# Attention of a graph layer: units taken in pairs, and the edge parts multiplied by their masks on VectorE

## The chip, the cores and the metric

One core of one Trainium2 chip. The metric is the device time of one execution in microseconds (us), the median of several. Engines as the profile names them: PE is TensorE, DVE is VectorE, ACT is ScalarE, POOL is GpSimd, SP is SyncE, which only issues transfers (SPq is its queue).

## The reference

A graph attention layer over 625 nodes and 20,000 edges sorted by their target, and behind it a layer of eight experts, two of them picked for each node, with a shared one. The change touches only the attention of the graph layer:

```python
logits = jnp.einsum('ehd,ehd->eh', q[src], k[dst])
a = logits + dist_attn + path_attn
mx = jax.ops.segment_max(a, dst, num_segments=N)
e = jnp.exp(a - mx[dst])
s = jax.ops.segment_sum(e, dst, num_segments=N)
sa = e / s[dst]
msg = v[src] * sa[:, :, None]
agg = jax.ops.segment_sum(msg, dst, num_segments=N).reshape(N, D)
```

There are 8 heads of 64 columns (D = 512).

## The kernel before

Attention is done densely. For a tile of 126 target nodes and one head, a **unit**, the kernel needs two matrices of 126 x 628 (targets by sources): the exponentials of the logits, and the sums of the edges' own factors (from the two edge inputs) for each pair of target and source. Five tiles times eight heads are 40 units. Their product, divided by its row sum, is the matrix of weights.

**Blocks.** The sums of the edges come from matmuls. Edges are cut into groups of three target nodes, four groups make a block, and there are 53 blocks (WB). For a block VectorE and GpSimd lay out the operands: VectorE makes four one-hots of the edges' sources (L946, 128 x 628 each, `onehot`) and a mask that says to which of a group's three nodes an edge belongs (L950, `mask`); GpSimd multiplies the edge parts by the mask (L926, `R`, in the profile group_weights: 128 partitions x 288 elements in bf16). TensorE multiplies the two (`sums`, L1045, 24 matmuls), ScalarE copies the result out of PSUM (`copied`, L1001) into one of three buffers, and SyncE stores it (L871) to a scratch tensor in HBM. From there SyncE loads each unit's rows (`unit_rows`, L881, sums_in).

**Windows.** The edges of a block come in by four small transfers (L168) into one of 8 slots. Their places in HBM depend on the data, so the issuing engine first loads them from a table into registers, four for a block. Even blocks are issued by SyncE, odd ones by GpSimd between its products (`load`). The first four are issued in the stage before, behind which SyncE issues the load of Wo.

**Units.** `logits` (L1055, for two units at once) on TensorE; `guards` (L959) on VectorE takes the row maximum; `exps` (L1007) on ScalarE; `weights` (L967) on VectorE multiplies sums and exponentials with the row sum, and takes the reciprocal (L970); `norm` (L1012) on ScalarE scales; `turn` (L1067) on TensorE transposes in five pieces; `keep` (L1017) on ScalarE copies them from PSUM; `weighted_sums` (L1077) on TensorE multiplies by the values for two units; `collect` (L975) on VectorE copies the result.

**Order.** Each engine's order is written out by hand and is fixed; engines wait for each other through counting semaphores. The first 14 blocks (`leading`) are summed before the first unit; VectorE lays out 16. From then on `blocks_by` gives 1.3 blocks to each unit until all are done at unit 30. VectorE does, for each unit, weights, at even ones a collect, the next unit's guards, then the next unit's blocks. ScalarE: norm, exps, keep, copies. TensorE: a block's sums, turn, logits or weighted sums, more sums. SyncE: the rows of two units ahead, then for each block a window's load, a wait for the block's copy, its store; in the last ten units also the four loads of W1 (1 MB each). A barrier ends the stage, and the next one starts with Wo.

## Time and profile before

| | us |
|---|---|
| median of 3 runs | 824.91 (824.5 to 826.6) |
| the profiled execution | 826.6 |
| its span, first to last instruction | 825.0 |
| TensorE busy in it | 700.9 |
| VectorE busy | 530.6 |
| ScalarE busy | 418.2 |
| GpSimd busy | 162.0 |

The profile is one execution. The time of an execution lies a little over its span. Times in the views are counted from the span's start. The attention stage lies between about 96 and 323 us; what comes before it prepares the edges and the projections, and what comes after are the feed-forward and the experts.

### The profile page before, as it was taken

The page shows a single profiled execution, that of the slowest core. Times are in us where ns is not written, and L with a number is a line of the kernel's source. Part 1 is how long each engine was busy: PE and PEld are TensorE (multiplying, and loading weights), DVE is VectorE, ACT ScalarE, POOL GpSimd, SP SyncE. Part 2 cuts the span into 40 slices and gives each one's busy share as a digit, 9 for nine tenths or more (in the row PEclk, how much of TensorE's full clock was granted, in tenths as well). Part 3 has the DMA queues.
Part 4 walks back from the last instruction along what each step waited for, and adds up shares of the span by engine and source line. Part 5 has one row for each costly group of instructions (what it writes and reads, how often), then busy time and mean ns, then how long its engine had stood idle before and what let it go on. Part 6 is the DMA issues. An engine that isn't in the chain of part 4 may idle for free. (4 is left out here: it accounts for less than half of the span.)

```text
span 825.0 us, 14610 instructions
## 1 busy us (share of the span) xinstructions
PE 700.9 (85%) x4978; PEld 550.0 (67%) x4978; DVE 530.6 (64%) x1109; ACT 418.2 (51%) x689; POOL 162.0 (20%) x240
## 2 busy tenths in 40 slices
PE   3987766776777764999999999999999999999993
PEld 2664333444555443479999679878889899888792
DVE  6737775788778543544422636338888788888854
ACT  4235333575656653373333543227666676676640
POOL 6341376455544103000000000400000000000022
PEclk9999965999989977999999999999999999999998
DMA  8633545656565581700001040957677677766124
GB/s 263 169 78 74 102 109 165 168 151 178 152 176 166 169 298 28 266 1 1 1 0 62 16 153 1 324 206 257 201 226 235 222 240 237 268 224 227 69 63 144
DMA packets 104157, 125.63 MB, mean 152 GB/s; under 512 B 32402, under 2 KB 70060, under 8 KB 103564
## 3 DMA queue, kind: packets, MB, share of 16 engines
q1 hardware_dynamic: 96955, 115.06, 43.9%
q0 software_dynamic: 5600, 6.54, 3.6%
q10 hardware_dynamic: 1520, 3.01, 1.6%
q8 instruction: 43, 0.70, 0.4%
q14 instruction: 39, 0.31, 0.1%
HBM read 94.91 MB, written 29.67 MB: 151 GB/s over the span
## 5 line engine op out<-in xcount | busy, mean ns | idle before, releaser
L2150 PE MATMUL ps<-xT,w_hi 128*128 128x480 f32 (+7 forms) x512 | 110.1, 337 | 2.3 <-DVE hT L1969 2.2
L2150 PEld LDWEIGHTS ps<-xT,w_hi 128*128 128x128 f32 x512 | 82.0, 189 | 9.9 <-DVE hT L1969 4.0
L1045 PE MATMUL ps<-onehot,group_weights 128*32 128x314 bf16 x1272 | 63.8, 347 | 26.3 <-POOL group_weights L926 8.6
L946 DVE TENSOR_SCALAR onehot<-iota_h,windows 128x628 bf16<-128x628 f16 x212 | 78.8, 433 | 4.1 <-PE ps L1045 4.0
L1955 DVE TENSOR_TENSOR w_lo<-weights_far,w_hi 128x1024 fp32r<-128x1024 f32 x64 | 77.9, 1219 | 2.5 <-ACT w_hi L2065 2.2
L2152 PEld LDWEIGHTS ps<-xT,w_lo 128*128 128x128 f32 x512 | 73.5, 190 | 1.6
L2152 PE MATMUL ps<-xT,w_lo 128*128 128x240 f32 (+7 forms) x512 | 74.5, 268 | 0.0
L1045 PEld LDWEIGHTS ps<-onehot,group_weights 128*32 128x32 bf16 x1272 | 38.6, 113 | 52.1 <-issue 28.4
L2065 ACT ACTIVATE w_hi<-weights_far 128x1024 fp32r<-128x1024 f32 x64 | 67.1, 1051 | 0.0
L168 POOL DMA_DIRECT2D windows<-window_scratch x104 | 58.8, 568 | 36.9 <-issue 30.9
L2175 PE MATMUL ps<-w_hi,hidden 128*128 128x512 f32 (+3 forms) x176 | 62.2, 405 | 2.7 <-DVE hidden L1979 1.9
L1001 ACT ACTIVATE sums_out<-ps 128x628 f32<-128x628 f32 x53 | 36.6, 691 | 46.8 <-PE ps L1045 43.2
L1941 POOL DMA_INDIRECT weights_far<-slot_results,gate x5 | 5.1, 1027 | 269.6 <-DMA slot_results<-weights_near 268.4
L1236 DVE TENSOR_TENSOR ff_hidden_lo<-ff_hidden,ff_hidden_hi 128x628 fp32r<-128x628 f32 x16 | 13.0, 812 | 66.1 <-ACT ff_hidden_hi L1320 66.1
L1067 PE MATMUL ps<-ident,weights 126*128 126x126 f32 (+1 forms) x200 | 33.6, 304 | 23.9 <-ACT weights L1012 22.0
L967 DVE CUSTOM_DVE_ANT_0 weights<-sums_in,exponents 126x628 f32<-126x628 f32 x40 | 33.7, 843 | 30.3 <-DMA sums_in<-sums_scratch 13.9
L926 POOL TENSOR_TENSOR group_weights<-windows,mask 128x288 bf16<-128x288 bf16 x53 | 40.3, 765 | 60.4 <-DVE mask L950 60.1
L1955 DVE TENSOR_TENSOR w_lo<-weights_near,w_hi 128x1024 fp32r<-128x1024 f32 x35 | 42.7, 1221 | 8.1 <-ACT w_hi L2065 8.1
L1012 ACT ACTIVATE weights<-weights,small 126x628 f32<-126x628 f32 x40 | 32.7, 817 | 29.2 <-DVE small L970 29.2
L1067 PEld LDWEIGHTS ps<-ident,weights 126*128 126x128 f32 (+1 forms) x200 | 23.1, 151 | 36.6 <-ACT weights L1012 30.4
L1317 ACT ACTIVATE ff_hidden<-ps,vs 128x314 f32<-128x314 f32 x32 | 16.6, 523 | 58.7 <-PE ps L1412 58.7
L1077 PE MATMUL ps<-weights_turned,vs 128*64 128x126 f32 (+1 forms) x400 | 31.6, 315 | 16.2 <-ACT weights_turned L1017 16.2
(309 smaller groups left out, 1544.6 us busy)
## 6 DMA issues: line engine op xcount, KB each, us to landing
weights_far<-in_L_ffn_w SPq DMA_DIRECT2D x64, 512.0 KB, 5.8
sums_scratch<-sums_out SPq DMA_DIRECT2D x53, 314.0 KB
weights_near<-in_L_ffn_w SPq DMA_DIRECT2D x32, 512.0 KB, 3.4
sums_in<-sums_scratch SPq DMA_DIRECT2D x40, 309.1 KB
weights_near<-in_L_gnn_W SPq DMA_DIRECT2D x4, 1024.0 KB, 6.5
weights_near<-in_L_ffn_sw SPq DMA_DIRECT2D x8, 512.0 KB, 5.1
weights_near<-in_L_gnn_Wqkv SPq DMA_DIRECT2D x3, 1024.0 KB, 7.8
weights_ff<-in_L_gnn_W SPq DMA_DIRECT2D x1, 3072.0 KB, 13.2
```

Of the source, the lines that this page charges most:

```text
L168: eng.dma_start(windows[:, w % RING, j, :], frm.rearrange("(p c) -> p c", p=P)).then_inc(g_in[w % RING], 16)
L926: pool.tensor_tensor(R[w % 3][:, :, 0:GD * H, :].rearrange("p j (d h) a -> p j d (h a)", h=H), parts[:, w % RING, :, 4:4 + 3 * H].unsqueez ...
L946: dve.tensor_scalar(onehot[w % 3][:, j, :], iota_h, windows[:, w % RING, j, 1:2], None, ALU.is_equal)\
L967: dve.tensor_tensor_reduce(PR[k][0:TILE], sums_in[u % 3][0:TILE], L[k][0:TILE], 1.0, 1e-37, ALU.mult, ALU.add, total[k][0:TILE]).then_inc( ...
L1001: act.activation(halves(sums_out[w % 3]), psW(w), ACT.Copy).then_inc(w_copied, 1)
L1045: last = pe.matmul(psW(w)[r, a, :], R[w % 3][:, j, :, part], onehot[w % 3][:, j, a * SH:(a + 1) * SH], start=part == 0, stop=part == 2)
L1067: last = pe.transpose(psP[0:n, t, 0:TILE], PR[u % 2][0:TILE, t * P:t * P + n], ident[0:TILE, 0:TILE])
L1955: dve.tensor_tensor(to[1], raw_rest[n] if v == V else raw[u][n], to[0], ALU.subtract)\
L2065: act.activation(to[0], raw_rest[n] if v == V else raw[u][n], ACT.Copy).then_inc(w_hi_ready, 1)
L2150: pe.matmul(both(bank, cap), w[u % 2][0][:, c, cut], xT(r)[:, c, :, :], start=c == 0, stop=False)
L2152: last = pe.matmul(bank[:, 0:cap], w[u % 2][1][:, c, cut], xT(r)[:, c, 0, :], start=False, stop=c == DC - 1)
L2175: last = pe.matmul(psum[4 + blk][0:rows, :], hid_parts[:, v % 2, m, at:at + rows], w2s[u][wp][:, m, :], start=first and i == 0, stop=final ...
```

## The change

- The product of edge parts and mask is made by VectorE (`products`), with the mask made one step ahead of it (`masks`, `products`, `onehots` in place of `group_weights`). GpSimd only issues its loads.
- The order of all engines goes by pairs of units (`PAIRS`), with 8 blocks to three pairs (`blocks_by`, `pair_blocks`); VectorE lays out two blocks ahead of TensorE (`laid_out`).
- Blocks 2 and 3 of every four are loaded by GpSimd, the others by SyncE (`by_pool`); the places of two blocks, eight registers, are loaded at once (`load_starts`). `place_at` gives the block whose load is issued with block w. Six blocks instead of four are loaded in the stage before.
- A unit's rows have four buffers instead of three, and are asked for by pairs.

```diff
-LOADED = 4
+LOADED = 6
...
-def blocks_by(unit):
-    return min(WB, window_blocks(0) + SPARE_BLOCKS + (13 * unit + 9) // 10)
...
-def unit_blocks(unit):
-    return range(blocks_by(unit), blocks_by(unit + 1)) if unit < UNITS_ALL else range(0)
+def blocks_by(pair):
+    return min(WB, window_blocks(0) + SPARE_BLOCKS + (8 * pair + 2) // 3)
+def pair_blocks(pair):
+    return range(blocks_by(pair), blocks_by(pair + 1))
+def laid_out(pair):
+    return range(min(WB, blocks_by(pair) + 2), min(WB, blocks_by(pair + 1) + 2))
...
...
+PAIRS = UNITS_ALL // 2
+def by_pool(w):
+    return w % 4 >= 2
+def place_at(w):
+    return [b for b in range(LOADED, 2 * WB) if by_pool(b)][w // 2], [b for b in range(LOADED, 2 * WB) if not by_pool(b)][w // 2]
+def load_starts(nc, engine, w, tab):
+    n = min(2 * GW, GROUPS - GW * w)
+    _, starts = nc.values_load_multi_w_load_instructions(tab[0:1, REL + GW * w:REL + GW * w + n], engines=[engine], min_val=0,
                                                          max_val=CHUNK * REC2)
+    return starts
+def load_groups(eng, w, starts, rec2_d, windows, g_in):
     for j in range(min(GW, GROUPS - GW * w)):
         b, k = divmod(GW * w + j, GPB)
         region = rec2_d[b, :, :].rearrange("e c -> (e c)")
-        frm = region[bass.ds(starts[j], P * REC2)] if k else region[0:P * REC2]
+        frm = region[bass.ds(starts[GW * (w % 2) + j], P * REC2)] if k else region[0:P * REC2]
         eng.dma_start(windows[:, w % RING, j, :], frm.rearrange("(p c) -> p c", p=P)).then_inc(g_in[w % RING], 16)
...
-            for w in range(0, LOADED, 2):
-                load_groups(nc, sp, mybir.EngineType.SP, w, tab, rec2_d, windows, g_in)
+            for w in range(LOADED):
+                if not by_pool(w):
+                    starts = load_starts(nc, mybir.EngineType.SP, w, tab) if w % 2 == 0 else starts
+                    load_groups(sp, w, starts, rec2_d, windows, g_in)
             sp.dma_start(wo[:, :, :], Wo.rearrange("(c p) n -> p c n", p=P)).then_inc(wo_in, 16)
...
-            for w in range(1, LOADED, 2):
-                load_groups(nc, pool, mybir.EngineType.Pool, w, tab, rec2_d, windows, g_in)
+            for w in range(LOADED):
+                if by_pool(w):
+                    starts = load_starts(nc, mybir.EngineType.Pool, w, tab) if w % 2 == 0 else starts
+                    load_groups(pool, w, starts, rec2_d, windows, g_in)
...
-        sums_in = [sb(f"sums_in{i}", [P, SRC]) for i in range(3)]
+        sums_in = [sb(f"sums_in{i}", [P, SRC]) for i in range(4)]
...
-            def load(w):
-                if w < WB and w % 2 == 0:
-                    wait_past(sp, windows_stored, stored_for(w))
-                    window_free(sp, w)
-                    load_groups(nc, sp, mybir.EngineType.SP, w, tab, rec2_d, windows, g_in)
-            def blocks(ws):
-                for w in ws:
-                    load(w + AHEAD)
-                    sp.wait_ge(w_copied, w + 1)
-                    sp.dma_start(sums_d[w, :, :], sums_out[w % 3]).then_inc(out_done[w % 3], 16)
+            starts = None
+            def block(w):
+                nonlocal starts
+                nxt = place_at(w)[1]
+                if w % 2 == 0 and nxt < WB:
+                    starts = load_starts(nc, mybir.EngineType.SP, nxt, tab) if nxt % 2 == 0 else starts
+                    wait_past(sp, windows_stored, stored_for(nxt))
+                    window_free(sp, nxt)
+                    load_groups(sp, nxt, starts, rec2_d, windows, g_in)
+                sp.wait_ge(w_copied, w + 1)
+                sp.dma_start(sums_d[w, :, :], sums_out[w % 3]).then_inc(out_done[w % 3], 16)
...
             def unit_rows(u):
                 tile, h = divmod(u, H)
                 if h == 0:
                     for i in range(3):
                         sp.wait_ge(out_done[i], 16 * len(range(i, window_blocks(tile), 3)))
-                wait_past(sp, summed, u - 2)
+                wait_past(sp, summed, u - 3)
                 g0 = tile * TILE // GD
                 rows = sums_d.rearrange("w (j d h) n -> (w j) d h n", j=GW, h=H)
-                sp.dma_start(sums_in[u % 3][0:TILE, :], rows[g0:g0 + TILE // GD, 0:GD, h, :]).then_inc(units_in[u % 3], 16)
...
-            for w in range(LOADED, AHEAD):
-                load(w)
-            blocks(range(window_blocks(0) + 1))
+                sp.dma_start(sums_in[u % 4][0:TILE, :], rows[g0:g0 + TILE // GD, 0:GD, h, :]).then_inc(units_in[u % 4], 16)
+            for w in range(window_blocks(0) + 1):
+                block(w)
             unit_rows(0)
             unit_rows(1)
-            blocks(range(window_blocks(0) + 1, leading))
-            for u in range(UNITS_ALL):
-                if u + 2 < UNITS_ALL:
-                    assert blocks_by(u) >= window_blocks((u + 2) // H)
-                    unit_rows(u + 2)
-                blocks(unit_blocks(u))
-                if UNITS_ALL - 10 <= u < UNITS_ALL - 2 and u % 2 == 0:
-                    load_w1(sp, W1, w_near, [(u - UNITS_ALL + 10) // 2], w1_in)
+            for w in range(window_blocks(0) + 1, leading):
+                block(w)
+            for q in range(PAIRS):
+                if q + 1 < PAIRS:
+                    assert blocks_by(q) >= window_blocks((2 * q + 2) // H)
+                    unit_rows(2 * q + 2)
+                    unit_rows(2 * q + 3)
+                for w in pair_blocks(q):
+                    block(w)
+                if PAIRS - 5 <= q < PAIRS - 1:
+                    load_w1(sp, W1, w_near, [q - PAIRS + 5], w1_in)
...
-            def load(w):
-                if w < WB and w % 2:
-                    wait_past(pool, windows_stored, stored_for(w))
-                    window_free(pool, w)
-                    load_groups(nc, pool, mybir.EngineType.Pool, w, tab, rec2_d, windows, g_in)
+            starts = None
             for w in range(WB):
-                pool.wait_ge(masked, w + 1)
-                wait_past(pool, w_ready, w - 2)
-                pool.tensor_tensor(R[w % 3][:, :, 0:GD * H, :].rearrange("p j (d h) a -> p j d (h a)", h=H),
-                                   parts[:, w % RING, :, 4:4 + 3 * H].unsqueeze(2).broadcast_to([P, GW, GD, 3 * H]),
-                                   mask[w % 2].unsqueeze(3).broadcast_to([P, GW, GD, 3 * H]), ALU.mult).then_inc(r_ready, 1)
-                load(w + AHEAD - 1)
+                nxt = place_at(w)[0]
+                if w % 2 == 0 and nxt < WB and nxt % 2 == 0:
+                    starts = load_starts(nc, mybir.EngineType.Pool, nxt, tab)
+                if w % 2 == 0 and nxt < WB:
+                    wait_past(pool, windows_stored, stored_for(nxt))
+                    window_free(pool, nxt)
+                    load_groups(pool, nxt, starts, rec2_d, windows, g_in)
...
-            def group_weights(w):
+            def masks(w):
                 dve.wait_ge(g_in[w % RING], groups_in(w))
-                wait_past(dve, w_ready, w - 2)
-                for j in range(GW):
-                    dve.tensor_scalar(onehot[w % 3][:, j, :], iota_h, windows[:, w % RING, j, 1:2], None, ALU.is_equal)\
-                       .then_inc(oh_ready, 1)
                 k0 = GW * w % GPB
                 wait_past(dve, r_ready, w - 1)
                 dve.tensor_tensor(mask[w % 2], windows[:, w % RING, :, 0:1].broadcast_to([P, GW, GD]),
                                   offsets[:, k0 * GD:(k0 + GW) * GD].rearrange("p (j d) -> p j d", d=GD), ALU.is_equal)\
                    .then_inc(masked, 1)
+            def products(w):
+                wait_past(dve, w_ready, w - 2)
+                dve.wait_ge(masked, w + 1)
+                dve.tensor_tensor(R[w % 3][:, :, 0:GD * H, :].rearrange("p j (d h) a -> p j d (h a)", h=H),
+                                  parts[:, w % RING, :, 4:4 + 3 * H].unsqueeze(2).broadcast_to([P, GW, GD, 3 * H]),
+                                  mask[w % 2].unsqueeze(3).broadcast_to([P, GW, GD, 3 * H]), ALU.mult).then_inc(r_ready, 1)
+            def onehots(w):
+                wait_past(dve, w_ready, w - 2)
+                for j in range(GW):
+                    dve.tensor_scalar(onehot[w % 3][:, j, :], iota_h, windows[:, w % RING, j, 1:2], None, ALU.is_equal)\
+                       .then_inc(oh_ready, 1)
...
-                dve.wait_ge(units_in[u % 3], 16 * (u // 3 + 1))
+                dve.wait_ge(units_in[u % 4], 16 * (u // 4 + 1))
...
-                dve.tensor_tensor_reduce(PR[k][0:TILE], sums_in[u % 3][0:TILE], L[k][0:TILE], 1.0, 1e-37, ALU.mult, ALU.add,
+                dve.tensor_tensor_reduce(PR[k][0:TILE], sums_in[u % 4][0:TILE], L[k][0:TILE], 1.0, 1e-37, ALU.mult, ALU.add,
...
-            for w in range(2):
-                group_weights(w)
-            guards(0)
-            for w in range(2, blocks_by(1)):
-                group_weights(w)
-            for u in range(UNITS_ALL):
-                weights(u)
-                if u % 2 == 0 and u:
-                    collect(u // 2 - 1)
-                if u + 1 < UNITS_ALL:
-                    guards(u + 1)
-                for w in unit_blocks(u + 1):
-                    group_weights(w)
-            collect(UNITS_ALL // 2 - 1)
+            masks(0)
+            for w in range(leading + 2):
+                products(w)
+                if w in (1, 2):
+                    guards(w - 1)
+                if w + 1 < leading + 2:
+                    masks(w + 1)
+                onehots(w)
+            for q in range(PAIRS):
+                ws = list(laid_out(q))
+                weights(2 * q)
+                if q:
+                    collect(q - 1)
+                weights(2 * q + 1)
+                for w in ws[0:1]:
+                    masks(w)
+                if q + 1 < PAIRS:
+                    guards(2 * q + 2)
+                for w in ws[0:1]:
+                    products(w)
+                    onehots(w)
+                for w in ws[1:2]:
+                    masks(w)
+                if q + 1 < PAIRS:
+                    guards(2 * q + 3)
+                for w in ws[1:2]:
+                    products(w)
+                for w in ws[2:]:
+                    masks(w)
+                for w in ws[1:2]:
+                    onehots(w)
+                for w in ws[2:]:
+                    products(w)
+                    onehots(w)
+            collect(PAIRS - 1)
...
-            for w in range(2):
+            for w in range(leading):
                 copied(w)
-            exps(0)
-            for w in range(2, leading):
-                copied(w)
-            for u in range(UNITS_ALL):
-                norm(u)
-                if u + 1 < UNITS_ALL:
-                    exps(u + 1)
-                keep(u)
-                for w in unit_blocks(u):
+                if w in (1, 2):
+                    exps(w - 1)
+            for q in range(PAIRS):
+                ws = list(pair_blocks(q))
+                norm(2 * q)
+                norm(2 * q + 1)
+                keep(2 * q)
+                for w in ws[0:1]:
+                    copied(w)
+                if q + 1 < PAIRS:
+                    exps(2 * q + 2)
+                keep(2 * q + 1)
+                for w in ws[1:2]:
+                    copied(w)
+                if q + 1 < PAIRS:
+                    exps(2 * q + 3)
+                for w in ws[2:]:
                     copied(w)
     @block.tensor
             logits(0)
             for w in range(leading):
                 sums(w)
-            for u in range(UNITS_ALL):
-                ws = list(unit_blocks(u))
+            for q in range(PAIRS):
+                ws = list(pair_blocks(q))
+                if q + 1 < PAIRS:
+                    logits(q + 1)
                 for w in ws[0:1]:
                     sums(w)
-                turn(u)
-                if u % 2 == 0 and u + 2 < UNITS_ALL:
-                    logits(u // 2 + 1)
-                if u % 2:
-                    weighted_sums(u // 2)
-                for w in ws[1:]:
+                turn(2 * q)
+                turn(2 * q + 1)
+                for w in ws[1:2]:
+                    sums(w)
+                weighted_sums(q)
+                for w in ws[2:]:
                     sums(w)
```

## Rows read from the trace of the kernel before

**Rows 1.** The windows view of two stretches: length, busy PE, PEld, DVE, ACT, POOL, clock

```profile
98.00:139.00 41.00, 23.82 (x360) 13.95 (x364) 27.34 (x80) 10.40 (x15) 30.02 (x48) 0.69 0.59 132
139.00:279.00 140.00, 103.23 (x1453) 69.10 (x1449) 108.86 (x319) 86.13 (x126) 64.60 (x101) 0.92 0.59 166
```

**Rows 2.** The order of time on GpSimd (POOL), leading part; start us, us, instruction

```profile
114.12 1.30 POOL L926 TENSOR_TENSOR group_weights<-windows,mask 128x288 bf16<-128x288 bf16 x2
...
121.40 0.63 POOL L168 DMA_DIRECT2D windows<-window_scratch  x1 [1.51 <-DVE onehot L946]
...
124.34 1.30 POOL L926 TENSOR_TENSOR group_weights<-windows,mask 128x288 bf16<-128x288 bf16 x2
```

**Rows 3.** The order of time on SyncE's queue (SPq), before and in the leading part

```profile
82.45 5.43 SPq L168 DMA_DIRECT2D windows<-window_scratch  x8
...
95.70 2.00 SPq L138 DMA_DIRECT2D window_scratch<-edge_parts  x2
101.65 5.41 SPq L168 DMA_DIRECT2D windows<-window_scratch  x8
...
132.85 0.91 SPq L871 DMA_DIRECT2D sums_scratch<-sums_out  x2
135.33 1.01 SPq L881 DMA_DIRECT2D sums_in<-sums_scratch  x1
```

**Rows 4.** The order of time on VectorE (DVE), the first weights

```profile
139.49 0.81 DVE L967 CUSTOM_DVE_ANT_0 weights<-sums_in,exponents 126x628 f32<-126x628 f32 x1 [3.58 <-DMA sums_in<-sums_scratch]
```

**Rows 5.** The order of time on VectorE (DVE), around unit 29

```profile
275.20 0.29 DVE L975 COPY hT<-ps 128x126 f32<-128x126 f32 x1 [1.43 <-PE ps L1077]
275.41 0.80 DVE L959 TENSOR_REDUCE small<-ps 126x1 f32<-126x628 f32 x1
276.12 1.25 DVE L946 TENSOR_SCALAR onehot<-iota_h,windows 128x628 bf16<-128x628 f16 x4
277.29 0.16 DVE L950 TENSOR_TENSOR mask<-windows,offsets 128x12 bf16<-128x12 f32 x1
277.37 0.80 DVE L967 CUSTOM_DVE_ANT_0 weights<-sums_in,exponents 126x628 f32<-126x628 f32 x1
...
278.45 0.81 DVE L959 TENSOR_REDUCE small<-ps 126x1 f32<-126x628 f32 x1
```

**Rows 6.** Groups of VectorE's instructions by form; count, busy us, mean ns, idle before

```profile
L1969 DVE TENSOR_TENSOR hT<-hT,ps 128x288 f32<-128x288 f32 x8 | 3.5, 443 | 0.0
...
L594 DVE TENSOR_TENSOR edge_parts<-records,edge_parts 128x400 bf16<-128x400 f32 x1 | 1.0, 958 | 0.5 <-ACT edge_parts L692 0.5
```

**Rows 7.** The instructions of line 168 on GpSimd; ns min/median/max

```profile
L168 POOL DMA_DIRECT2D windows<-window_scratch x104: 534/534/1257, 82.9 to 258.3; - x104
```

**Rows 8.** The order of time on SyncE's queue in units 0 to 29

```profile
204.12 0.91 SPq L881 DMA_DIRECT2D sums_in<-sums_scratch  x1
205.98 0.35 SPq L871 DMA_DIRECT2D sums_scratch<-sums_out  x1
208.16 1.88 SPq L168 DMA_DIRECT2D windows<-window_scratch  x4
```

**Rows 9.** The order of time, all engines, units 30 to 39

```profile
280.22 0.81 DVE L967 CUSTOM_DVE_ANT_0 weights<-sums_in,exponents 126x628 f32<-126x628 f32 x1 [0.95 <-ACT exponents L1007]
...
310.35 0.82 ACT L1012 ACTIVATE weights<-weights,small 126x628 f32<-126x628 f32 x1 [0.59 <-DVE small L970]
...
311.22 0.76 PE L1067 MATMUL ps<-ident,weights 126*128 126x126 f32 x5 [0.67 <-ACT weights L1012]
...
312.87 1.30 PE L1077 MATMUL ps<-weights_turned,vs 128*64 128x126 f32 x20 [0.89 <-ACT weights_turned L1017]
...
318.53 1.26 PE L1067 MATMUL ps<-ident,weights 126*128 126x126 f32 x5 [3.15 <-ACT weights L1012]
...
320.58 2.37 PE L1077 MATMUL ps<-weights_turned,vs 128*64 128x126 f32 x20 [0.79 <-ACT weights_turned L1017]
323.00 0.29 DVE L975 COPY hT<-ps 128x126 f32<-128x126 f32 x1 [5.37 <-PE ps L1077]
```

4 lines of the change are left out of this document (1 added, 3 removed).

## Prediction

> **What bounds the kernel now.** I read the busy time by stretches first, then the order of time inside each stretch, since the change lies in one stage that runs from about 97 to 323 us. The stage has three parts with different limits. The first stretch (98 to 139 us) is the leading part: 14 blocks are summed before the first unit. GpSimd is the busiest engine there, 30.02 of 41.00 us, and TensorE was granted 0.69 of its full clock on the mean, so for much of it the lower of its two levels, 1.2 GHz [rows 1]. In the order of time GpSimd repeats itself every 10.22 us (114.12 to 124.34) for four blocks: four products, two bursts of four load issues, and register loads in front of a burst (1.51 us of the gap before 121.40) [rows 2]. It is never idle for long, so it sets 2.56 us a block. SyncE stores block 11 by 133.76 us, issues the first unit's rows at 135.33 [rows 3], and VectorE, idle for 3.58 us, starts the first weights at 139.49 [rows 4].
>
> In the second stretch (units 0 to 29, 139.49 to 280.22, 140.7 us for 30 units and their blocks) no engine is full: VectorE is busy 108.86 of 140.00 us, TensorE 103.23, ScalarE 86.13, GpSimd 64.60 [rows 1]. The time goes into turns between engines: each unit's chain runs alone. In the third (units 30 to 39, no blocks left, 280.22 to 323.29, 43.1 us) only that chain is left [rows 9].
>
> **The change part by part.** *The product moves from GpSimd to VectorE, 53 times.* The trace has no such product on VectorE. The nearest row by size is an addition of 288 elements, 443 ns [rows 6]; an operation starts about 0.09 us before the one in front ends (a reduction of 0.80 us holds the engine for 0.71) [rows 5], so I take 0.36 us. From above: another with two-byte elements and strided operands took 958 ns for 400 elements [rows 6], so 0.69 and 0.60 us of engine. From below: no less than 0.2 us, since the mask with its 12 elements already lasts 0.16 [rows 5]. I choose the 288-element row, since the product reads its parts and writes its result contiguously, as that one does; the other strides. A block then costs VectorE 0.08 for the mask, 0.36, and 1.17 for the four one-hots, 1.61 us [rows 5].
>
> A rule bears on the lower bound. The row says 0.443 us for 288 elements of four bytes, and the product has two. By the Trainium skill (Vector Engine (DVE) Microarchitecture Reference, section 5.1) a two-source operation on two-byte data doubles its rate only if every operand's innermost step is one, and the mask is read with step zero here. By that rule 0.36 stands; at double rate it would be about 0.2, and the sum would fall by 37 times 0.16, 5.9 us.
>
> The product adds two waits on VectorE: for its own mask, with another operation laid between, and for the sums of three blocks before. Behind the second stand the block's one-hots and the next unit's reduction, and ScalarE's exponentials wait for those; three blocks back TensorE is done by then (below).
>
> *Loads.* GpSimd only issues, and runs ahead as slots come free. SyncE has the same number of bursts, but takes eight registers at once for two windows. Now four registers cost the gap from 206.33 to 208.16, 1.83 us; eight cost between that and 3.66; I take 3.0, since part must be per register. A burst of four issues is 1.9, a store 0.45, a unit's rows 0.95 [rows 8].
>
> *Before the stage.* SyncE now ends its window loads at 87.88 and issues Wo. It gets 8 more issues, 3.8 us ((5.43 less some 1.6 for the registers between) over 8 each), 1.2 for a longer first register load, 3.0 for a second: it ends near 96.3, and the stage's first transfer now starts at 95.70 [rows 3]. So the stage starts 1.0 later (0 to 2). Behind these issues stands Wo's load, wanted only after the stage.
>
> *The leading part.* GpSimd leaves the path. VectorE would need 16 blocks of 1.61 and two reductions, 27.2 us, ending near 125 to 126. SyncE is later: its first burst starts at 101.65 plus 1.2 plus 1.0, 103.85; blocks 0 to 3 need two bursts and four stores, 5.6; blocks 4 to 11 twice 3.0 plus 5.6. It issues the store of block 11 by 126.7, against 133.76 now. From there the same 5.73 us to the first weights: 132.4. That is 7.1 us less. With registers at 3.66 and bursts at 2.7 it is 139.2, no gain; with registers at 1.83 and no late start it is 127.9, 11.6 less. What is late next is SyncE, whose stores free the three output buffers.
>
> *Units 0 to 29, in pairs.* By the new order each engine has two units' work between its waits. I laid one pair of three blocks out: weights at 0 and 1.3, reductions at 2.4 and 5.0; ScalarE scales at 1.1 and 2.4, keeps at 3.3 and 5.5, exponentiates at 4.7 and 6.9; TensorE's weighted sums end at 7.5. Every wait of VectorE's is met before VectorE comes to it. So VectorE's own work sets it: 15 pairs of two weights (2.16), a collect (0.21) and two reductions (1.42), 56.9 us, and the 37 blocks not yet laid out at 1.61, 59.6: 116.4 us [rows 5]. TensorE with its 103.23 and ScalarE with its 86.13 fit below. SyncE needs, for four blocks (1.5 pairs), 3.0 + 3.8 + 1.8 + 2.85 = 11.45 us, 115 us in all [rows 8]. Two in-order queues this near to full won't run without gaps: VectorE is idle 22% of this stretch now [rows 1], and I keep half that share: 130 us, 10.7 less. With the product at 0.60 it is 10 us more, at 0.2 about 6 less.
>
> *Units 30 to 39.* The chain that repeats per pair runs from a collect to the next: to the odd unit's weights 0.21, to its scaling's end 1.05 and 0.82, keep of the even unit 0.7, turning of the odd and its keep 1.65 (311.22 to 312.87), weighted sums 1.33: 5.76 us [rows 5, 9]. Four pairs at that, and 8.2 from the last pair's start to its collect, are 31.2 us. At the lower clock turning takes 1.26 for 0.76 and the weighted sums 2.37 for 1.30 [rows 9], 1.57 more a pair; for half of the five pairs, 3.9. So 35.1 us for 43.1, 8.0 less (4 to 11.6). The four loads of W1 lie in this part; a unit's rows are now asked for four units ahead, not three, which covers them.
>
> The fourth sums buffer and the later place of Wo's load cost nothing: both lie beside other work. Behind the stage nothing changes, as a barrier ends it.
>
> Sum: 7.1 + 10.7 + 8.0 = 25.8 us less. The profiled execution took 826.6 us (span 825.0); 800.8 then, and against the median of 824.91, 799.1. I say 800.
>
> **The rivals.**
> *The pairs bring little and the product is dear.* At 0.60 us of engine the second stretch needs VectorE for 116.4 + 37 x 0.24 = 125.3 us, with the same share of gaps 140: no gain there, and 810 us. For it speaks the 958 ns row [rows 6], against it that row's strides.
> *SyncE becomes the bound.* Registers at 3.66, bursts at 2.7: 13.7 us for four blocks, 137 us, and its rows come late; leading part as now. Then only 4 and 8 us are gained: 813. For it speaks that a wait on a copy holds all behind it in SyncE's queue, and that 8 issues with the registers between took 5.41 us at 101.65 [rows 3]; against it, that its registers are fetched half as often.
> *The chains don't overlap in fact* (the change doesn't do what it says): a wait that I didn't see keeps the second and third stretch as they are; only the 7.1 us remain: 818.
> *Slower: GpSimd's load issues starve.* VectorE works with hardly a gap, and GpSimd's issue must get in between. An issue takes 534 ns in the median and 1257 at most today [rows 7]. GpSimd needs 8 issues and some 2.2 us of registers for four blocks. It decides from 1.7 us an issue: then four blocks take 15.8 us, the stretch 158, 17 over now, which eats the other gains. At 2.0 us it is 182 us for the stretch, about 26 us over now in all: 851. Against it: in units 0 to 29 issues lay beside one-hots all the time at 0.53.
>
> On this the Trainium skill (SBUF — State Buffer, Who interferes with whom) says that VectorE's two-port modes lock GpSimd out of writing its descriptors, and the same page (A bandwidth-pool intuition that's wrong) has an issue of about 0.62 us taking about 3.1 beside such a copy; by it the stretch would be near 270 us. The rows, with their maximum of 1.257, don't show it.
>
> **How the numbers follow.** Chances: forecast 0.52; product nearly twice as fast (794 us) 0.08; product dear 0.12; SyncE 0.10; no overlap 0.08; slower 0.06; several of these at once, worth about nothing, 0.04, of it 0.03 within 0.3%. Within the forecast SyncE's registers (7 us) and the clock in the third stretch (4) give 793 to 808. The range must take in the dear product and SyncE as bound, and goes to 816; below, the fast product in part: 792. Under 0.3% (2.5 us) is what a measurement of this kernel can't tell from no change. So faster 0.90, same 0.03, slower 0.07.
>
> **What would show it.** In the profile after: first weights near 132 us, VectorE's product near 0.45 us long, GpSimd under 20% busy in the stage; weights of unit 30 some 130 us after the first, VectorE over 85% busy between; the last collect 35 us later. Wrong it would be by a product over 0.65 us, by SyncE's register load over 3.5 us with VectorE waiting for a unit's rows, by load issues over 1.3 us, or by pairs of more than 7 us in the third stretch.

## Result, and the profile after

The changed kernel takes 817.47 us (median of 5, 812.19 to 819.45) where the kernel before, measured beside it, takes 824.5 (median of 5, 822.4 to 826.6): ratio 0.9895, interval 0.9854 to 0.9936. It is faster by 7 us, not by 25. The profiled execution is the fastest of the five: 812.19 us, span 810.2, against 826.6 and 825.0 before.

Four points in the order of time divide the difference of the spans: first weights, weights of unit 30, last collect, and the first transfer of the stage behind. In short the first four lines are called head, units, tail and gap.

| part | before | forecast | after |
|---|---|---|---|
| to the first weights | 139.49 | 132.4 | 138.32 |
| units 0 to 29 | 140.7 | 130 | 128.6 |
| units 30 to 39, to the last collect | 43.1 | 35.1 | 35.9 |
| last collect to the next stage | 4.7 | 4.7 | 10.8 |
| the rest of the span | 497.0 | 497.0 | 496.5 |

So 1.2 + 12.1 + 7.2 - 6.1 + 0.5 = 14.9 us (the spans differ by 14.8). Two lines of the table are off, the first and the fourth.

The windows view of the kernel after, as [rows 1] (the last two columns are the busy share of the transfer engines and GB/s); the third stretch is units 30 to 39, the fourth the way to the next stage:

```profile
98.00:138.00 40.00, 25.15 (x378) 14.18 (x376) 27.53 (x96) 11.05 (x16) 22.37 (x40) 0.74 0.84 167
138.00:268.00 130.00, 100.79 (x1474) 67.42 (x1474) 113.50 (x359) 88.19 (x129) 33.04 (x56) 0.92 0.62 184
268.00:302.00 34.00, 23.38 (x184) 16.99 (x182) 15.87 (x40) 20.31 (x28) 2.67 (x3) 0.82 0.75 215
302.00:314.00 12.00, 0.84 (x8) 0.42 (x4) 0.35 (x2) 0.32 (x1) 3.48 (x3) 0.50 0.01 2
```

GpSimd falls from 64.60 to 33.04 us in the units, VectorE is busy 113.50 of 130 us, 87%. In the leading part GpSimd falls from 30.02 to 22.37 us, and the transfers' share goes from 0.59 to 0.84. In the last stretch next to nothing is busy for 12 us.

The order of time on SyncE's queue, after, in front of and in the leading part, as [rows 3]:

```profile
94.80 0.43 SPq L451 DMA_DIRECT2D wo<-in_L_gnn_Wo  x1
95.64 4.99 SPq L138 DMA_DIRECT2D window_scratch<-edge_parts  x2
105.10 1.91 SPq L193 DMA_DIRECT2D windows<-window_scratch  x4
107.06 0.90 SPq L901 DMA_DIRECT2D sums_scratch<-sums_out  x2
108.20 2.86 SPq L193 DMA_DIRECT2D windows<-window_scratch  x4
111.11 2.30 SPq L901 DMA_DIRECT2D sums_scratch<-sums_out  x2
116.23 1.87 SPq L193 DMA_DIRECT2D windows<-window_scratch  x4
...
121.33 0.90 SPq L901 DMA_DIRECT2D sums_scratch<-sums_out  x2
126.30 1.88 SPq L193 DMA_DIRECT2D windows<-window_scratch  x4
...
131.34 0.90 SPq L901 DMA_DIRECT2D sums_scratch<-sums_out  x2
133.93 1.88 SPq L911 DMA_DIRECT2D sums_in<-sums_scratch  x2
```

Three things differ from the forecast. The two stores right behind Wo's load hold the queue for 4.99 us instead of 2.00 [rows 3], and the first burst (four window loads) starts at 105.10, not 103.85. The first four blocks take 8.3 us (to 113.41), not 5.6. Registers for eight places cost 2.82 us (113.41 to 116.23) and 4.07 (122.23 to 126.30) against 3.0. The last store is issued by 132.24, forecast 126.7.

VectorE in the order of time, after, as [rows 4]: end of its leading blocks, first weights, weights of unit 30, last collect:

```profile
129.18 1.25 DVE L990 TENSOR_SCALAR onehot<-iota_h,windows 128x628 bf16<-128x628 f16 x4
138.32 0.81 DVE L1006 CUSTOM_DVE_ANT_0 weights<-sums_in,exponents 126x628 f32<-126x628 f32 x1 [7.89 <-DMA sums_in<-sums_scratch]
...
266.96 0.81 DVE L1006 CUSTOM_DVE_ANT_0 weights<-sums_in,exponents 126x628 f32<-126x628 f32 x1 [2.79 <-DMA sums_in<-sums_scratch]
...
302.58 0.29 DVE L1014 COPY hT<-ps 128x126 f32<-128x126 f32 x1 [6.12 <-PE ps L1145]
```

VectorE is done with 16 blocks at 130.4 and waits 7.89 us for the first rows of sums. The product and GpSimd's issues by instruction (ns min/median/max), as [rows 6, 7]:

```profile
L982 DVE TENSOR_TENSOR group_weights<-windows,mask x53: 442/449/459, 97.5 to 258.6; 128x288 bf16<-128x288 bf16 x53
...
L193 POOL DMA_DIRECT2D windows<-window_scratch x104: 534/534/1319, 83.7 to 234.1; - x104
```

The last things before the next stage, in the order of time on SyncE and GpSimd, before and then after:

```profile
312.52 7.26 POOL L932 TENSOR_TENSOR xs<-xs,output_biases 128x512 f32<-128x512 f32 x5 [33.81 <-DMA ff_columns<-in_L_gnn_ln_b]
...
327.96 0.31 SPq L1158 DMA_DIRECT2D gate_work<-in_L_ffn_gate_w  x1
```

```profile
284.69 0.43 SPq L930 DMA_DIRECT2D output_biases<-in_L_gnn_bo  x1
...
286.80 0.28 SPq L934 DMA_DIRECT2D ff_columns<-in_L_gnn_ln_b  x1
...
299.33 6.14 POOL L960 TENSOR_TENSOR xs<-xs,output_biases 128x512 f32<-128x512 f32 x5 [64.65 <-DMA ff_columns<-in_L_gnn_ln_b]
...
313.66 0.31 SPq L1228 DMA_DIRECT2D gate_work<-in_L_ffn_gate_w  x1
```

GpSimd adds bo to the rows of xs once five small loads have landed. SyncE issues them last, behind W1, at 284.69 to 286.80; they land at 299, so the additions end at 305.47, after the last collect (302.87), and the stage behind starts 8.2 us after that. Before, the additions ended at 319.78, 3.5 us ahead of the last collect (323.29), and the stage behind started 8.2 us after them as well. So they already set the end of the stage there; only 4.7 us of it showed.

### The profile page after: what moved, and what is told of

Read it like the earlier page. It is cut to its first block and busy times, and to the rows that moved or that the text cites. A ratio compares the mean times of both kernels' runs of the same rounds, so it can differ in the third digit from the quotient of the medians.

```text
span 810.2 us, 14580 instructions
## 1 busy us (share of the span) xinstructions
PE 696.5 (86%) x4978; PEld 547.9 (68%) x4978; DVE 532.6 (66%) x1162; ACT 417.8 (52%) x689; POOL 121.8 (15%) x187
## 5 line engine op out<-in xcount | busy, mean ns | idle before, releaser
L1113 PE MATMUL ps<-onehot,group_weights 128*32 128x314 bf16 x1272 | 59.7, 331 | 15.8 <-DVE onehot L990 8.2
L990 DVE TENSOR_SCALAR onehot<-iota_h,windows 128x628 bf16<-128x628 f16 x212 | 66.8, 378 | 0.0
L1113 PEld LDWEIGHTS ps<-onehot,group_weights 128*32 128x32 bf16 x1272 | 34.6, 109 | 39.3 <-DVE onehot L990 16.1
L775 PE MATMUL ps<-hT,weights_near 128*128 128x320 f32 x128 | 38.6, 465 | 1.6 <-ACT hT L667 1.6
L2245 PEld LDWEIGHTS ps<-w_hi,hidden 128*128 128x128 f32 (+3 forms) x176 | 31.9, 181 | 11.1 <-DVE hidden L2049 2.5
```

The source lines that it names most:

```text
L775: last = pe.matmul(psum[i % 4][:, 0:HALF], wqkv[:, c, m * P:(m + 1) * P], hT[:, c, half * HALF:(half + 1) * HALF], start=c == 0, stop=c == ...
L990: dve.tensor_scalar(onehot[w % 3][:, j, :], iota_h, windows[:, w % RING, j, 1:2], None, ALU.is_equal)\
L1113: last = pe.matmul(psW(w)[r, a, :], R[w % 3][:, j, :, part], onehot[w % 3][:, j, a * SH:(a + 1) * SH], start=part == 0, stop=part == 2)
L2245: last = pe.matmul(psum[4 + blk][0:rows, :], hid_parts[:, v % 2, m, at:at + rows], w2s[u][wp][:, m, :], start=first and i == 0, stop=final ...
```

## Experiments

Medians with range and count; the ratio is to the kernel before, measured beside it. "Head", "units", "tail", "gap" are the first four lines of the table, read from the one profiled execution. A part of the head's scatter lies in front of the stage, so where it matters the head is also counted from SyncE's first window load (82.45 before, 83.42 after): that length is 57.0 us before (55.7 in a second profile with the head of before), and 54.6 to 55.4 in the seven profiles here whose head is that of the kernel after.

**The changed kernel again.** Nothing edited.

> The changed kernel once more, as the base of this call. The five executions on record lay between 812.2 and 819.5 us. I expect a median of 814 to 819, and in the profile the same stretches within a few us: first weights at 138.3, 128.6 us to unit 30, 35.9 to the last collect, 10.8 to the next stage.

816.15 us (813.34 to 818.28, 4), ratio 0.9891 (0.9828 to 0.9953). Head 138.84, units 131.4, tail 35.7, gap 11.1. Two executions of one kernel differ by 3 us in the units; a difference of less than that in one profile is weak evidence by itself.

**Pairs alone**: the product back on GpSimd, behind its window loads. **Product alone**: the kernel before with only the product on VectorE, behind the one-hots, and the mask ahead of them. The cut shows the first.

```diff
-                dve.wait_ge(masked, w + 1)
-                dve.tensor_tensor(R[w % 3]..., ALU.mult).then_inc(r_ready, 1)
...
+                pool.wait_ge(masked, w + 1)
+                wait_past(pool, w_ready, w - 2)
+                pool.tensor_tensor(R[w % 3]..., ALU.mult).then_inc(r_ready, 1)
```

> The pairs alone: the changed kernel, but GpSimd makes the product, between its loads, as in the kernel before. Theory: VectorE's work in the pairs falls by 37 times 0.37, 13.7 us, but its one-hots lengthen again beside GpSimd's products and GpSimd's in-order loads wait for masks. Units 0 to 29 take 128 to 136 us, not less, since SyncE's and the transfers' share is what is left: the same as the changed kernel or up to 6 us slower. Rival: VectorE's own work bounds the pairs, and taking the product off it gains 5 us or more.

> The product alone: the kernel before in its order of units, with the product made by VectorE behind the one-hots, and GpSimd only issuing loads. Theory: the leading part, then bound by SyncE and VectorE and not GpSimd, gets 2 to 5 us shorter; units 0 to 29 stay near 140 us, as turns between engines bound them: within 5 us of the kernel before. Rival: the product's move is what gains, and this is 8 us or more faster than before.

Pairs alone: 815.61 (813.0 to 816.89, 4), ratio 0.9865 (0.9802 to 0.9929). Product alone: 826.25 (10 runs), ratio 1.0012 (0.9977 to 1.0047). All of the gain comes from the rest of the change: the pairs, the order of the loads and the fourth buffer together, which no run here takes apart. The move costs little because it pays for half of itself: 53 products add 23.8 us (449 ns each) to VectorE's rows, and its 212 one-hots, which took 433 ns on the mean beside GpSimd's products, take 378 without them, 78.8 us of busy time down to 66.8. In all VectorE's busy time rises by 4.2 us in the kernel before (530.6 to 534.8) and by 6.6 under the pairs (526.0 to 532.6). Nor did GpSimd's products set the head: counted from the first window load it is 57.1 us without them in the order of before, and 54.95 with them in the order of after.

**Biases first**: the five loads ahead of W1's, in the kernel after and in the kernel before.

```diff
+                if q == PAIRS - 5:
+                    bias_loads()
                 if PAIRS - 5 <= q < PAIRS - 1:
                     load_w1(sp, W1, w_near, [q - PAIRS + 5], w1_in)
...
```

> The changed kernel with the five small loads of the biases and columns (bo, b2, b1 and two more) issued ahead of the four loads of W1 instead of behind them. My theory: the stage ends when GpSimd has added bo, which waits for these loads, and the next stage starts 8.2 us after GpSimd's last addition (before: 319.78 to 327.96; after: 305.47 to 313.66). With the loads early, GpSimd's additions end some 20 us before the last collect, and from the last collect (302.87) to the next stage's first instruction it takes less than 4.7 us, the smallest seen, instead of 10.8: the time falls by 6 to 8 us against the changed kernel, to about 810. The rival, that the gap follows from the last collect or from the W1 loads' end, expects the gap to stay above 8 us and the time within 2 us of the changed kernel.

> The same edit on the kernel before. If GpSimd's additions set the end there too (319.78 plus 8.2 is 327.96), the gap from the last collect to the next stage, 4.7 us, shrinks, by 0 to 4 us, and the time falls by as much. If not, nothing moves.

Kernel after: 808.46 (806.74 to 809.56, 4), ratio 0.9788 (0.9742 to 0.9834); gap 1.3, tail 40.5. Kernel before: 826.63 (10), ratio 1.001 (0.9981 to 1.0039); gap 1.3, tail 47.7. The order of time with biases first, GpSimd, VectorE and SyncE:

```profile
279.88 6.15 POOL L966 TENSOR_TENSOR xs<-xs,output_biases 128x512 f32<-128x512 f32 x5 [43.66 <-DMA ff_columns<-in_L_gnn_ln_b]
...
285.31 1.38 DVE L1012 CUSTOM_DVE_ANT_0 weights<-sums_in,exponents 126x628 f32<-126x628 f32 x1 [7.50 <-DMA sums_in<-sums_scratch]
...
310.13 0.33 SPq L1234 DMA_DIRECT2D gate_work<-in_L_ffn_gate_w  x1
```

The gap closes, but 4.6 us come back in the tail, where the pair of units 34 and 35 waits 7.50 us for rows. In the kernel before, whose gap hung on the same additions, the two just cancel: 3.4 us out of the gap, 4.6 into the tail.

**Who pays in the tail.** The additions beside that pair, or the loads? In the kernel with stores on ScalarE and biases first (below), the additions cover 2 of 512 columns and leave the rest of bo out.

```diff
-            pool.tensor_tensor(xs[:, t, :], xs[:, t, :], rows_b[:, 0:D], ALU.add)
+            pool.tensor_tensor(xs[:, t, 0:2], xs[:, t, 0:2], rows_b[:, 0:2], ALU.add)
```

> The kernel with the two edits (stores on ScalarE, biases ahead of W1), in which GpSimd's five additions of bo cover 2 of 512 columns, so that they take almost no time; the rest of bo is left out. Theory (the last ten units take 4.6 us more with the biases ahead of W1 because rows of sums land later behind these transfers): the pair of units 34 and 35 still starts 11 to 12 us after the pair in front, the last ten units still take 40 to 41 us, and the time stays within 1.5 us of 804.8. Rival (the additions, which lie beside that pair and in which its first weights took 1.38 instead of 0.81 us, hold VectorE or the loads): the last ten units take 36 us and the time falls by 3 to 5 us.

804.74 (801.22 to 805.96, 4), ratio 0.9748 (0.9696 to 0.9799); tail 40.1, that pair 11.6 us behind the one in front, as with the additions whole (11.8). So it is not the additions but the loads. The order of time on SyncE and VectorE around this pair's rows, in the kernel after and with biases first alone:

```profile
268.87 1.63 SPq L911 DMA_DIRECT2D sums_in<-sums_scratch  x2
270.55 0.55 SPq L825 DMA_DIRECT2D weights_near<-in_L_gnn_W  x1
271.14 1.64 SPq L911 DMA_DIRECT2D sums_in<-sums_scratch  x2
...
281.18 0.81 DVE L1006 CUSTOM_DVE_ANT_0 weights<-sums_in,exponents 126x628 f32<-126x628 f32 x1 [2.98 <-DMA sums_in<-sums_scratch]
```

```profile
270.05 1.63 SPq L920 DMA_DIRECT2D sums_in<-sums_scratch  x2
...
274.35 2.34 SPq L920 DMA_DIRECT2D sums_in<-sums_scratch  x2
```

The pair's rows (the second sums_in line) are fully issued 2.3 us after the rows in front of them in the kernel after, and 5.0 us after them with the five bias loads between. From there to the pair's weights it takes 8.4 us (272.78 to 281.18) and 8.6 (276.69 to 285.31). So of the 3 us or so by which this pair comes later, most is its place in SyncE's queue, behind five more issues, and not a slower landing.

**W1 amid the units**: its four parts behind pairs 3, 7, 11 and 15.

```diff
-                if PAIRS - 5 <= q < PAIRS - 1:
-                    load_w1(sp, W1, w_near, [q - PAIRS + 5], w1_in)
+                if q in (2, 6, 10, 14):
+                    load_w1(sp, W1, w_near, [(q - 2) // 4], w1_in)
```

> The changed kernel with the four loads of W1 (4 MB) issued one each behind pairs 2, 6, 10 and 14 in place of pairs 15 to 18. Theory: the last ten units are bound by their rows' landing behind W1 (VectorE waits 1.9 to 3.0 us for each pair there), and the late landing of the biases, which holds GpSimd, is also W1's doing. Then the last part takes 31 to 33 us in place of 35.9, GpSimd's additions end before the last collect, and the gap of 10.8 us to the next stage shrinks to under 3; the pairs with W1 may each take 1 to 2 us more: 10 to 13 us faster than the changed kernel in all. Rival: the rows' latency itself (issue, store, read back) is the wait, and W1 matters not: last part at 35 or more.

811.15 (809.21 to 812.31, 4), ratio 0.9814 (0.9752 to 0.9876). Gap 1.5, but units 138.5; the tail stays at 35.5. The pair behind the first part, in the order of time on SyncE and VectorE:

```profile
168.29 0.46 SPq L825 DMA_DIRECT2D weights_near<-in_L_gnn_W  x1
...
177.87 0.81 DVE L1006 CUSTOM_DVE_ANT_0 weights<-sums_in,exponents 126x628 f32<-126x628 f32 x1 [3.90 <-DMA sums_in<-sums_scratch]
```

This pair starts 12.9 us after the one in front, 8.9 and 9.6 in the two executions of the kernel after: 1 MB in the path of the rows costs 3 to 4 us.

**SyncE's registers twice** in the leading part, and **ScalarE issues the leading stores**:

```diff
+                    if w < 12 and nxt % 2 == 0:
+                        starts = load_starts(nc, mybir.EngineType.SP, nxt, tab)
```

```diff
-                sp.wait_ge(w_copied, w + 1)
-                sp.dma_start(sums_d[w, :, :], sums_out[w % 3]).then_inc(out_done[w % 3], 16)
+                if w >= leading:
+                    sp.wait_ge(w_copied, w + 1)
+                    sp.dma_start(sums_d[w, :, :], sums_out[w % 3]).then_inc(out_done[w % 3], 16)
...
+                if w < leading:
+                    act.wait_ge(w_copied, w + 1)
+                    act.dma_start(sums_d[w, :, :], sums_out[w % 3]).then_inc(out_done[w % 3], 16)
```

> The changed kernel with SyncE's eight-register loads of blocks 0, 4 and 8 done twice (three more of them). Theory A: three times 3.4 us in SyncE's queue, so the first weights come 7 to 10 us later, near 147, and the rest is shifted. Theory B: under 3 us.

> The changed kernel, but the stores of the first 14 blocks are issued by ScalarE right behind its copies, so that SyncE issues only windows there. Theory A, SyncE's queue (eight registers at about 3.4 us, bursts, stores in line) sets the first weights at 138.3: they come at 129 to 132, bounded by VectorE, which ended its 16 blocks at 130.4; the time falls by 6 to 8 us. Theory B, the landing time of the stores (3.3 us median, up to 5.5) in busy transfer engines sets it: they come at 136 or later, and the time falls by under 3 us.

Registers twice: 817.37 in a single execution, head 144.16, 5.3 and 5.8 us later than in the two executions of the kernel after; counted from the first window load it is 61.9 us and 7.0 more, for three loads of registers. Stores on ScalarE: 807.15 (804.84 to 811.21, 4), ratio 0.9765 (0.9718 to 0.9812); head 135.30, and SyncE issues the first rows at 127.0 instead of 133.9, which land 8.3 us later. With 54.9 us from the first window load in the kernel after, this is 51.5, and 48.1 to 49.9 in four more kernels with the same head (with the additions cut, and the first three lines of the table below). So SyncE's queue holds the head, and behind it the transfers; 135.3 lies between the ranges of both theories. The median lies 9 to 10 us under the changed kernel's, and this profile, the slowest of its four, shows 3 to 3.5 us of it; where the rest lies is not shown.

**Wo's load later**, behind the third pair instead of in front of the stage.

```diff
-            sp.dma_start(wo[:, :, :], Wo.rearrange("(c p) n -> p c n", p=P)).then_inc(wo_in, 16)
+            LATE["wo"] = lambda sp: sp.dma_start(wo[:, :, :], Wo.rearrange("(c p) n -> p c n", p=P)).then_inc(wo_in, 16)
...
+                if q == 2:
+                    LATE["wo"](sp)
```

> The changed kernel with the 1 MB load of Wo issued behind the third pair instead of ahead of the stage. Theory (the leading part is held by the landing of transfers, whose share of the span is 0.84 in it): about 1 MB less stands ahead of the sums, so the first weights start some 2 us sooner than 138.3 us and the time falls by 1 to 3 us against the changed kernel. Rival (SyncE's own queue sets the first weights, whatever the transfers do): the first weights stay within 0.5 us of 138.3 and the time stays within 1 us, less the 0.1 us of one issue. Other rival (the load collides with the units' rows once it is later): the first weights come sooner and the 30 leading units grow by as much.

812.29 (808.85 to 812.86, 4), ratio 0.9832 (0.9792 to 0.9871). The order of time on SyncE and VectorE:

```profile
93.91 1.87 SPq L141 DMA_DIRECT2D window_scratch<-edge_parts  x2
101.04 1.90 SPq L196 DMA_DIRECT2D windows<-window_scratch  x4
...
132.38 0.81 DVE L1013 CUSTOM_DVE_ANT_0 weights<-sums_in,exponents 126x628 f32<-126x628 f32 x1 [6.61 <-DMA sums_in<-sums_scratch]
```

Without Wo in front the two stores hold the queue for 1.87 us, the first burst comes 7.1 us behind their start instead of 9.5, and the first weights at 132.38. Of the 5.9 us, 1.3 are an earlier start of the window loads (82.16 against 83.42), which the edit doesn't touch, and some 4.6 are Wo: 50.2 us from the first window load, against 54.6 to 55.4. That 132.38 is also the number forecast is partly chance: without the earlier start it would be near 133.6, and from the first burst on it takes 31.3 us where 28.5 were forecast. 3 to 4 us come back in the units, where the pair that then waits starts 12.9 us after the one in front, against 8.9 and 9.6; the units as a whole are 132.9, the tail 38.3 and 2.4 to 2.7 more.

**The edits together.** Stores on ScalarE with biases first; the same with the biases behind the fifth pair; stores on ScalarE with W1 behind pairs 3, 6, 9, 12 and biases behind pair 14; and the first of these with Wo later.

> The changed kernel with both edits that gained alone: the five bias loads ahead of W1's (808.5 alone), and the leading blocks' stores issued by ScalarE (807.2 alone). Theory (two places, the gap before the next stage and the head of the stage, that don't touch): both gains add up, 8 and 9 us off 816.2, so 800 to 803. Rival (both only free the same transfers' time, and the profiles show no more than 3 us of the second gain at the head): 804 to 807.

> As the run before, but the five bias loads are issued behind the fifth pair, amid the 30 leading units, and W1 stays where the changed kernel has it. Theory (the tail grew by 4.6 us with the biases ahead of W1 because the transfers there were full, and GpSimd's additions took VectorE's port or the biases' packets delayed the sums): the tail is again 36 us, the gap before the next stage stays closed at 1.3 us, and 3 to 5 us more are gained: 797 to 800. Rival (the biases delay the units' loads wherever they stand): the 30 units grow by 2 to 4 us and the time stays that of the run before.

> The changed kernel with the stores of the leading blocks on ScalarE, W1's four parts behind pairs 3, 6, 9 and 12, and the biases behind pair 14. Theory (what W1 costs amid the units was its transfers' time, 7 to 10 us over 30 units with parts behind pairs 3, 7, 11 and 15): the units again take 136 to 139 us, the tail 35, the gap 1.5, and the time is 806 to 810, worse than with W1 left in the tail. Rival (in the other order it was mostly the run's own scatter): units 130 to 132 and 798 to 801.

> The changed kernel with three edits: the leading blocks' stores on ScalarE, the five bias loads ahead of W1's, and Wo's load behind the third pair. Theory (a transfer of 1 MB costs 4 to 6 us of the stage wherever it stands, so moving Wo only moves its price; the head is held by both SyncE's queue and the transfers): first weights at 129 to 131 us, the pair in which Wo lands 3 to 4 us longer, time 803 to 806, no better than the two edits alone (804.8). Rival (with SyncE's queue relieved too, what Wo costs at the head is more than what it costs amid the units): first weights near 127 and 799 to 802.

| kernel | us (range, runs) | ratio (interval) | head | units | tail | gap |
|---|---|---|---|---|---|---|
| stores, biases first | 804.76 (802.63 to 807.27, 6) | 0.9757 (0.9728 to 0.9787) | 133.5 | 130.2 | 40.9 | 1.3 |
| stores, biases behind pair 5 | 807.51 (804.76 to 810.74, 6) | 0.9799 (0.9767 to 0.9830) | 132.7 | 138.6 | 35.6 | 1.3 |
| stores, W1 and biases amid | 804.32 (801.59 to 805.21, 4) | 0.9751 (0.9715 to 0.9788) | 130.8 | 137.3 | 33.4 | 1.3 |
| stores, biases first, Wo later | 799.58 (796.04 to 801.96, 6) | 0.9698 (0.9657 to 0.9738) | 128.7 | 129.2 | 40.4 | 1.3 |

What leaves tail or gap for the units is paid there, in the second line not by loads alone: the longest of its pairs, 15.2 us, is the one beside GpSimd's additions (last section). Only the head's two edits add up (45.5 us from the first window load, 9.4 less than in the kernel after, of it 4.7 by Wo and 3.4 to 6.8 by the stores), and the forecast's 800 us is reached with edits that the change doesn't have. My theory that Wo's price merely moves fell: it costs more in the head than amid the units, where the pair behind it takes 11.6 us against 8.9 to 10.0. Of what was on record for the others, the rival's range held in the first line (804 to 807 us), its direction in the second (the units grew by 8 us where it had 2 to 4), and in the third the units came as the theory had them, with the time 2 us under its range.

**What sets the units.** The product made twice (the first time into a spare tile), and a product that covers one group of four and leaves three quarters of the edge parts out:

```diff
+                dve.tensor_tensor(mask[2 + w % 3]..., ALU.mult)
                 dve.tensor_tensor(R[w % 3]..., ALU.mult).then_inc(r_ready, 1)
```

```diff
-                dve.tensor_tensor(R[w % 3][:, :, 0:GD * H, :]..., ALU.mult).then_inc(r_ready, 1)
+                dve.tensor_tensor(R[w % 3][:, 0:1, 0:GD * H, :]..., ALU.mult).then_inc(r_ready, 1)
```

> The changed kernel in which VectorE makes every product twice, the first time into a spare tile: 0.37 us more of VectorE for each of 53 blocks, 13.7 us for the 37 beside units 0 to 29. Theory (VectorE's own work sets those units, as the prediction has it): from the first weights to those of unit 30 it takes 141 to 145 us instead of 128.6 to 131.4, and the time is 828 to 831. Rival (pairs that wait for sums have slack on VectorE, and only the other pairs feel it): 4 to 8 us more there, 820 to 824. The leading part, held by SyncE and the transfers, doesn't move.

> The changed kernel in which the product covers one of a block's four groups, so that three quarters of the edge parts are left out of the sums; the product is then 0.15 to 0.2 us long instead of 0.45, some 0.25 us less of VectorE a block, 9 us for the 37 beside units 0 to 29. Theory (VectorE's work sets those units): 120 to 122 us instead of 128.6 to 131.4, 807 us. Rival (the landing of sums and the turns between engines set most pairs): 2 to 4 us less there, 812 to 814.

Twice: 818.3 (813.68 to 819.73, 10), ratio 0.9922 (0.9894 to 0.995), units 132.1. A quarter (224 ns each): 817.02 (813.75 to 824.23, 10), ratio 0.9908 (0.9873 to 0.9943), units 132.2. The windows view of the units, twice and then a quarter:

```profile
140.00:272.00 132.00, 100.99 (x1464) 67.23 (x1466) 125.36 (x394) 87.90 (x129) 30.95 (x56) 0.92 0.61 180
```

```profile
140.00:272.00 132.00, 103.36 (x1482) 68.80 (x1482) 105.86 (x358) 87.41 (x130) 32.26 (x56) 0.91 0.61 181
```

VectorE's work goes from 105.86 to 125.36 us in the same 132: it is not what sets this part. What changes in its place is its wait for rows of sums behind the first weights: 20.8 us with a quarter, 12.5 in the kernel after, 5.4 with two products. Both numbers that I had put on record for the double product, 141 to 145 us and 4 to 8 us more, were too high. SyncE is the candidate left: it loads registers in the gaps between its rows. The order of time on SyncE in the units, kernel after, as [rows 8]:

```profile
191.36 2.13 SPq L193 DMA_DIRECT2D windows<-window_scratch  x4
193.54 1.22 SPq L901 DMA_DIRECT2D sums_scratch<-sums_out  x2
194.80 1.76 SPq L911 DMA_DIRECT2D sums_in<-sums_scratch  x2
196.82 2.81 SPq L193 DMA_DIRECT2D windows<-window_scratch  x4
199.67 1.51 SPq L901 DMA_DIRECT2D sums_scratch<-sums_out  x2
204.46 2.12 SPq L193 DMA_DIRECT2D windows<-window_scratch  x4
...
209.82 1.89 SPq L193 DMA_DIRECT2D windows<-window_scratch  x4
```

Of the 13.1 us from 191.36 to 204.46 issues take 9.4 and the gap with the loads of eight registers 3.3 (201.18 to 204.46); 0.4 us are left. Whether a part of that gap is also a wait the rows don't tell.

**SyncE's queue longer and shorter in the units**: its registers loaded twice from block 16 on (eight times), and the stores of all blocks on ScalarE, in the kernel with three edits.

> The changed kernel in which SyncE loads the eight registers twice for the eight bursts that it issues from block 16 on, beside the units; the leading part is as it was. Theory (SyncE's queue sets units 0 to 29): 8 times 3.3 us, 20 to 27 us more between the first weights and those of unit 30, 836 to 842. Rival (that queue has slack there and the turns between engines set the pairs): under 8 us more, up to 824.

> The kernel with three edits (799.6), in which ScalarE issues the stores of all 53 blocks, not of the leading ones alone. Theory (SyncE's in-order queue, full with register loads, bursts, stores and rows, sets units 0 to 29): 37 stores of some 0.45 us and the waits on copies leave that queue, those units take 112 to 120 us instead of 129.2, and the time is 785 to 792. Rival (the time from a store to the rows that are read back, and not the queue, sets them): no more than 4 us less there, 796 to 800. Other rival (a store's issue on ScalarE delays the exponentials): the same or slower, 800 to 806.

Longer: 832.57 (831.34 to 835.89, 10), ratio 1.0078 (1.0053 to 1.0103); units 148.1, 16.7 and 19.5 us more than in the two executions of the kernel after, for eight loads of registers. One costs some 2.8 us: the gap is 3.3 to 3.7 us in six places of the kernel after and 6.0 to 6.9 in five places here. One of them, in the order of time on SyncE:

```profile
195.05 1.65 SPq L913 DMA_DIRECT2D sums_in<-sums_scratch  x2
202.66 1.92 SPq L193 DMA_DIRECT2D windows<-window_scratch  x4
```

Shorter: 789.33 (787.49 to 793.58, 6), ratio 0.9546 (0.9511 to 0.9581), against 0.9698 with SyncE storing. So of some 22 us put into SyncE's queue about three quarters or more arrive: it has little slack, and it sets most of this part. Neither range on record held (20 to 27 us more, or under 8). The shorter one is the best version run, 37 us under the kernel before. How much the shorter queue gives there the profile leaves open: units 126.3 and 2.9 us less, with VectorE's wait for rows down from 13.9 to 3.8 us, but that execution was the slowest of its six, 4 us over their median. The time lies where the theory had it (785 to 792), the units where its rival had them (no more than 4 us less; the theory said 112 to 120). VectorE is then busy for 113.2 of the 126.3 us, so it can't be far from the next limit.

## Why the prediction was wrong

The measured time lies above the range. By its own steps:

- **"The fourth sums buffer and the later place of Wo's load cost nothing."** This step failed for Wo. Put off by the eight extra window loads from their old end, 87.88 [rows 3], to 94.80, its 1 MB went right in front of the stage's first stores. With Wo out of the way the first weights come at 132.38, with it at 138.3 and 138.8; some 4.6 us of that are Wo's, and the rest lies in the leading part, next.
- **The leading part otherwise.** SyncE as the next limit was right. That GpSimd's products held it before was not: without them the head stayed (product alone), and 54.95 us with them on GpSimd again equal the kernel after. The stage's start I took 1.0 late: its first transfer was not late (95.64), its first burst came 3.45 us later than before, where I had 2.2. Per four blocks 8.8 and 10.0 us instead of 8.6; eight registers 2.8 to 4.1, within and over my bounds (1.83 to 3.66); the product 0.36 of engine as forecast.
- **"Behind the stage nothing changes, as a barrier ends it."** Failed. I named what W1's later rows might do to the units and not what stands behind W1 in the same queue. Sooner collects didn't bring sooner biases, and the gap grew by 6.1 us. No rival held this. The rows of before already had it: its stage, too, ended 8.2 us behind GpSimd's additions.
- **Units 0 to 29.** 130 forecast, 128.6 and 131.4 measured: the number was right and its reason was not. That is luck. "VectorE's own work sets it" fell by the two product runs; the rival in which SyncE becomes the bound had the mechanism and too high a price (137 us), and register loads of its kind are what the run with the longer queue adds. That VectorE was 87% busy proved nothing.
- **Units 30 to 39.** 35.1 forecast, 35.9 and 35.7 measured. That rows asked for four units ahead cover W1 holds only in part: VectorE waits 1.9 to 3.0 us for rows in each of the four last pairs, 9.9 us in all, which the sum put at nothing. With W1 and the biases amid the units the part took 33.4, so little of that wait counts here; with the biases in front of W1 it takes 4.6 us more.
- **Product.** 449 ns, forecast 0.45. The Trainium skill (Vector Engine (DVE) Microarchitecture Reference, section 5.1) asks for innermost steps of one in every operand for the double rate, and the trace agrees that there was none: from 72 to 288 elements the product grows from 224 to 449 ns, 1.04 ns an element, and the four-byte row of [rows 6] has the same 443 ns for 288. The dear product falls as a rival twice: it wasn't dear, and even twice its length costs nothing that can be told.
- **GpSimd's issues.** 534 ns in the median and 1319 at most, not starved, with VectorE 87% busy. That GpSimd would be under 20% busy in the stage was wrong as these rows count: 33.04 of 130 us in the units, 22.37 of 40 in the head, its issues among them.
- **The median.** Profile against profile it is 14.4 us, median against median 7.0. One execution of each is not the kernel: the profiled one was the lowest of five after and the highest before. The median of its repetition is 9 us under the kernel before. The parts of the other kernels are read from one execution each in the same way. Executions of one kernel spread by 3 to 12 us, and a part of that goes with TensorE's granted clock: 0.92 in the units of this profile and 0.88 in those of the repetition, where they took 2.8 us more, and of the executions of the kernel before measured beside the experiments the five shortest (819.2 to 821.0 us) have 0.951 to 0.956 on the mean, the five longest (829.7 to 831.4) 0.941 to 0.948. Whether the clock causes the spread is not shown, and the five of the changed kernel don't order by it.

So of the 25.8 us, 5.9 failed in the head and 6.1 in the gap, units, tail and the rest gave 1.1 more than forecast, which makes 14.9; the other 7 to 8 are the difference between these two executions and the medians.

## What to carry to other kernels

When a change makes an engine's queue longer in front of a load, look at what that load now runs into: issued 7 us later, 1 MB stood in the path of small transfers on which the whole stage waited, and cost 4.6 us. When a stage gets shorter, ask of each thing that is wanted at its end, small ones too, whether it also comes sooner; five small loads behind 4 MB ate 6 us. And a queue that shows gaps may be full: SyncE's register loads are no rows, and twenty microseconds more or less on the "87% busy" engine did nothing, while eight register loads more cost 17 to 19 us.
